# Turning the masks by DMA instead of on TensorE, and late one-hots in two full-width buffers, in a neighbour-maximum kernel

## What is computed

```python
h = maximum(layernorm(x), 0)
mask = adj != 0
vals, idx = top_k(where(mask, -arange(1024), -inf), 25)   # the first 25 neighbours of a row
feats = where(valid, h[idx], -inf)
agg = feats.max(axis=2)
agg = where(degree <= 25, maximum(agg, 0), agg)
out = x + relu(concat([h, agg]) @ W + b)
```

## Time and profile before

| | us |
|---|---|
| median of 3 runs | 699.37 (698.42 to 699.73) |
| the profiled execution | 697.45 |
| its span, first to last instruction | 695.7 |
| PE busy | 630.9 (91%) |
| DVE busy | 613.7 (88%) |
| ACT busy | 472.3 (68%) |
| POOL busy | 50.3 (7%) |

### The profile page before, as it was taken

One profiled execution on the slowest core, in us unless ns is written; L12 is line 12 of the kernel. 1 busy time (PEld: TensorE's weight loads), 2 busy tenths in 40 slices (PEclk: granted clock), 3 DMA queues, 4 the chain that ended last, 5 costly groups with the idle time before them and its releaser, 6 DMA issues.

```text
span 695.7 us, 10819 instructions
## 1 busy us (share of the span) xinstructions
PE 630.9 (91%) x3376; PEld 297.4 (43%) x3376; DVE 613.7 (88%) x813; ACT 472.3 (68%) x642; POOL 50.3 (7%) x41
## 2 busy tenths in 40 slices
PE   2479998999989999899999999899999999999976
PEld 2133443535445354443545344353535335353423
DVE  3368999899998999989998899989998899988997
ACT  2689478783777639775795947777497927959120
POOL 1300021000210002100030002100021000300000
...
GB/s 361 199 87 27 60 152 68 182 70 16 152 73 200 60 15 136 83 188 60 128 23 122 151 60 151 68 196 57 41 122 87 185 60 32 16 107 1 60 15 16
DMA packets 19127, 67.64 MB, mean 97 GB/s; under 512 B 4499, under 2 KB 7830, under 8 KB 16534
## 3 DMA queue, kind: packets, MB, share of 16 engines
...
## 4 chain that ended last, share of the span: by engine, by line
PE 66%; DVE 16%; issue 10%; ACT 4%; DVEq 1%; DMA 1%; POOL 1%; ACTq 0%
PE picked L506 18%; PE picked L507 17%; PE ring L455 14%; DVE late_hot L684 4%; PE side L469 4%; PE ring L449 4%; DVE hot L659 4%; PE side L463 4%; DVE best L775 3%; DVE best L678 3%; PE final L534 2%; PE final L538 2%; PE final L491 1%; DMA adj_in<-in_adj_dram 1%; DVEq L771 1%
## 5 line engine op out<-in xcount | busy, mean ns | idle before, releaser
L678 DVE TENSOR_TENSOR best<-picked,best 128x1024 f32<-128x1024 f32 x224 | 270.5, 1218 | 38.2 <-PE picked L507 36.0
L506 PE MATMUL picked<-hot,h_hi 128*128 128x512 f16 x512 | 194.5, 380 | 15.0 <-DVE best L775 7.5
L507 PE MATMUL picked<-hot,h_lo 128*128 128x512 f16 x512 | 194.0, 379 | 0.0
L506 PE MATMUL picked<-late_hot,hi_skew 128*128 128x512 f16 x336 | 127.6, 380 | 13.1 <-DVE late_hot L684 8.2
L507 PE MATMUL picked<-late_hot,lo_skew 128*128 128x512 f16 x336 | 127.3, 379 | 0.0
L344 ACT ACTIVATE late_rank<-ring,late_bias 128x512 bf16<-128x512 f32 x128 | 81.4, 690 | 57.6 <-PE ring L455 57.6
L775 DVE TENSOR_TENSOR best<-picked,best 128x1024 f32<-128x1024 f32 x84 | 102.4, 1219 | 8.3 <-PE picked L507 8.2
L378 ACT COPY best<-picked 128x1024 f32<-128x1024 f32 x32 | 32.2, 1013 | 102.6 <-PE picked L507 102.6
L659 DVE TENSOR_SCALAR hot<-rank 128x4096 f16<-128x4096 bf16 x64 | 89.4, 1399 | 12.0 <-ACT rank L344 12.0
L349 ACT ACTIVATE past<-side,bias_cut 128x512 bf16<-128x512 f32 x128 | 88.3, 690 | 6.2 <-PE side L469 4.9
L344 ACT ACTIVATE rank<-ring,bias_big 128x512 bf16<-128x512 f32 x128 | 83.1, 692 | 5.2 <-PE ring L455 4.9
...
## 6 DMA issues: line engine op xcount, KB each, us to landing
adj_in<-in_adj_dram SPq DMA_DIRECT2D x16, 2048.0 KB, 7.7
...
```

Source lines behind the costliest of these rows:

```text
L506: nc.tensor.matmul(dst, hi[:, slot, k, :], onehot, start=start, stop=False)
L507: return nc.tensor.matmul(dst, lo[:, slot, k, :], onehot, start=False, stop=stop)
L678: nc.vector.tensor_tensor(best[:, half, s, :, :], picked[s][:, :, :], best[:, half, s, :, :], ALU.max).then_inc(picked_read, 1)
```

## The change

The names and lines of the kernel after are some ten lines further down; what belongs together:

- **Masks by DMA.** The 32 PE transposes of a group and ACT's four copies go. ACT makes all four masks of a group in one go (`make_masks`), reading the int32 input with a stride of 8 elements so that the classes come out packed, and SP turns them with four transposing DMAs (`turn_masks`) into one of two buffers `mask_t`. The masks of group g+3 are made and turned in step g, one step earlier than before.
- **Places.** `lower_sums` moves from behind use 4 to the end of the step before it. The late ranks stand with uses 4 to 9 instead of 5 to 8, the prefix sums with 4 to 11, the ranks with 9 to 14, DVE's `count_rounds` behind take 11 instead of 9, the first late one-hot behind take 12 instead of 10 and 11.
- **Late one-hots.** They are full width (128 x 4096) and lie in two of four buffers `hot`. The one for round r+1 is made at the head of round r.
- **Prologue.** `x` is loaded first, then the first group's `adj` in four parts. DVE makes the first group's masks and the parts of `h` (before: ACT and POOL), and the masks of group 1 come from ACT.

```diff
-    LATE_WITH, PREFIX_WITH, RANK_WITH = spread_over(5, 8), spread_over(5, 12), spread_over(9, 13)
-
-    LATE_HOT_USES, COUNT_USE, MASK_USES = (10, 11), 9, (4, 9)
+    LATE_WITH, PREFIX_WITH, RANK_WITH = spread_over(4, 9), spread_over(4, 11), spread_over(9, 14)
+
+    LATE_HOT_USE, COUNT_USE = 12, 11
...
+    FIRST_RING = K
+    RING = 2 * K
+    LATE_AT, RANK_AT = 0, K
+    TURNED = 16 * Q
...
-            load_adj(0, 0)
+            masks_due = sp.alloc_register("sp_masks_due")
+            sp.reg_mov(masks_due, 0)
+
+            def turn_masks(slot):
+
+                sp.reg_add(masks_due, masks_due, Q)
+                for q in range(Q):
+                    sp.wait_ge(mask_made, q + 1)
+                    if q == 0:
+                        sp.wait_ge(mask_made, masks_due)
+                    sp.dma_start_transpose(mask_t[:, slot, :, q * P:(q + 1) * P],
+                                           mask[:, q, :, :].rearrange("p k j -> p (k j)")).then_inc(mask_turned, 16)
+
             load_x(0)
+            for q in range(Q):
+                sp.dma_start(adj_in[:, 0, q * N:(q + 1) * N], adj_v[0][:, q * N:(q + 1) * N]).then_inc(adj_first[q], 16)
             load_adj(1, 1)
             sp.dma_start(w_in[:, :, :], W.rearrange("(s p) n -> p s n", p=P)).then_inc(weights_loaded, 16)
             for i in range(3):
                 sp.dma_start(bias_in[i:i + 1, :], b.rearrange("(a n) -> a n", a=1)).then_inc(weights_loaded, 16)
             load_xres(0, 0)
-            for g in (0, 1):
-                sp.wait_ge(mask_made, Q * (g + 1))
-                load_adj(g + 2, g)
+            sp.reg_add(masks_due, masks_due, Q)
+            for q in range(Q):
+                sp.wait_ge(mask_made, q + 1)
+                sp.dma_start_transpose(mask_t[:, 0, :, q * P:(q + 1) * P],
+                                       mask[:, q, :, :].rearrange("p k j -> p (k j)")).then_inc(mask_turned, 16)
+            load_adj(2, 0)
+            turn_masks(1)
+            load_adj(3, 1)
             skew_h(0, 0)
             skew_late(0)
+            turn_masks(0)
...
+                if not at_end(it, u, 3):
+                    turn_masks((u + 1) % 2)
...
+                if isinstance(batch, int) and batch == 0:
+                    pool.wait_ge(mask_made, Q)
...
+            def make_masks(slot):
+
+                act.reg_add(turned_due, turned_due, TURNED)
+                act.reg_add(adj_due[slot], adj_due[slot], 16)
+                act.wait_ge(mask_turned, TURNED)
+                act.wait_ge(mask_turned, turned_due)
+                act.wait_ge(adj_loaded[slot], adj_due[slot])
+                for q in range(Q):
+                    counts = adj_in[:, slot, q * N:(q + 1) * N].bitcast(U32).rearrange("p (j k) -> p k j", k=K)
+                    nc.scalar.activation(mask[:, q, :, :], counts, ACT.Sign).then_inc(mask_made, 1)
...
-            relu_parts(0, 0)
...
+            stage(0, K - 1, rank[:, 0], bias_big[:, 0:1])
+            make_masks(1)
             turned_h(0, 0)
-            find_late(0, 0, FIRST_RING - TURNS)
+            find_late(0, 0, FIRST_RING)
...
+            make_masks(0)
...
-                    if use in MASK_USES and not at_end(it, u, 2):
-                        make_mask(MASK_USES.index(use), u % 2, 16 * (it * (UNROLL // 2) + u // 2 + 2), at)
...
-                if not at_end(it, u, 2):
-                    for q in range(len(MASK_USES), Q):
-                        make_mask(q, u % 2, 16 * (it * (UNROLL // 2) + u // 2 + 2), at)
...
-                if not at_end(it, u, 2):
-                    for n in range(TURNS):
-                        turned_mask(at + TURN_AT, n)
+                if not at_end(it, u, 3):
+                    make_masks((u + 1) % 2)
...
-            def turn_mask(g, at, n):
-                if n == 0:
-                    pe.wait_ge(mask_made, Q * (g + 1))
-                take(at + n)
-                for j in range(2):
-                    for q in range(Q):
-                        last = nc.tensor.transpose(ring16[n % 2][:, j, q * P:(q + 1) * P], mask[:, q, 2 * n + j::K], eye[:, :])
-                last.then_inc(ring_written, 1)
...
+            def lower_sums(g, half):
+
+                pe.wait_ge(mask_turned, TURNED * (g + 1))
...
+            def late_hot_of(turn, k):
+                return hot[:, bass.ds(1 + turn, 1), k, :]
...
+                    turn = nc.s_assert_within(r % 2, 0, 1, skip_runtime_bounds_check_because="a remainder of two")
+                    pe.wait_ge(late_hot_made, done + (r + (g + 1)))
...
-                        pe.wait_ge(late_hot_made[s], done + (r + (g + 1)))
                         pe.wait_ge(late_read[s], done + r + 1)
...
-                                last = pick(picked[s][:, j, :], hi_skew, lo_skew, k, late_hot[:, k, :], slot, i == 0, i == LINK - 1)
+                                last = pick(picked[s][:, j, :], hi_skew, lo_skew, k, late_hot_of(turn, k), slot, i == 0, i == LINK - 1)
                         last.then_inc(late_written[s], 1)
...
-                if not at_end(it, u, 2):
-                    turn_mask(g + 2, at + TURN_AT, 0)
                 if more:
                     pick_pair(g + 1, 2, next_slot)
+                    pick_pair(g + 1, 3, next_slot)
+                project(g, it, u, new_batch)
                 if not at_end(it, u, 2):
-                    turn_mask(g + 2, at + TURN_AT, 1)
-                if more:
-                    pick_pair(g + 1, 3, next_slot)
-                if not at_end(it, u, 2):
-                    turn_mask(g + 2, at + TURN_AT, 2)
-                    turn_mask(g + 2, at + TURN_AT, 3)
-                project(g, it, u, new_batch)
+                    lower_sums(g + 2, u % 2)
...
+            def first_mask(q):
+
+                dve.wait_ge(adj_first[q], 16)
+                nc.vector.tensor_scalar(mask[:, q, :, :], adj_in[:, 0, q * N:(q + 1) * N].rearrange("p (j k) -> p k j", k=K),
+                                        0.0, None, ALU.not_equal).then_inc(mask_made, 1)
+
+            def first_parts():
+
+                dve.wait_ge(normed_made, 1)
+                nc.vector.tensor_scalar(h_hi[:, 0, :, :], h32[:, :, :], 0.0, None, ALU.max).then_inc(h_made, 1)
+                dve.wait_ge(h_made, 1)
+                nc.vector.tensor_scalar(h32[:, :, :], h32[:, :, :], 0.0, None, ALU.max).then_inc(h_made, 1)
+                dve.wait_ge(h_made, 2)
+                nc.vector.tensor_tensor(h_lo[:, 0, :, :], h32[:, :, :], h_hi[:, 0, :, :], ALU.subtract).then_inc(lo_made, 1)
...
-                nc.vector.tensor_scalar(hot[:, (t - 1) % 3, :, :], rank[:, s, :, :], float(t), None,
+                nc.vector.tensor_scalar(hot[:, t - 1, :, :], rank[:, s, :, :], float(t), None,
...
-            def make_late_hot(i, which):
-
-                part = slice(i * HALF, (i + 1) * HALF)
-                nc.vector.tensor_scalar(late_hot[:, part, :], late_rank[:, part, :], which, None,
-                                        ALU.is_equal).then_inc(late_hot_made[i], 1)
+            def make_late_hot(turn, which):
+
+                nc.vector.tensor_scalar(hot[:, turn, :, :], late_rank[:, :, :], which, None, ALU.is_equal).then_inc(late_hot_made, 1)
...
-            for q in range(Q):
-                make_mask(q, 0, 16, None)
             stats_of(0, range(K))
             moments_of(0)
+            first_mask(0)
+            make_gain(0)
+            for q in range(1, Q):
+                first_mask(q)
...
-            make_gain(0)
-            for q in range(Q):
-                make_mask(q, 1, 16, TURNS)
-            dve.wait_ge(ring_read, FIRST_RING - TURNS)
-            make_hot(1, 0)
-            make_hot(2, 0)
...
+            first_parts()
+            dve.wait_ge(ring_read, FIRST_RING)
+            make_hot(1, 0)
+            make_hot(2, 0)
...
-                    if use in LATE_HOT_USES:
+                    if use == LATE_HOT_USE:
                         dve.wait_ge(ring_read, at + RANK_AT)
-                        make_late_hot(LATE_HOT_USES.index(use), numbers[:, 1:2])
+                        make_late_hot(1, numbers[:, 1:2])
...
-                    dve.wait_ge(ring_read, at + TURN_AT)
+                    dve.wait_ge(ring_read, at + RING)
                     make_hot(1, 1 - s)
...
+                    turn = nc.s_assert_within((r + 1) % 2, 0, 1, skip_runtime_bounds_check_because="a remainder of two")
+                    make_late_hot(bass.ds(1 + turn, 1), numbers[:, bass.ds(r + 2, 1)])
                     for i in range(2):
                         dve.wait_ge(late_written[i], done + r + 1)
                         nc.vector.tensor_tensor(best[:, s, i, :, :], picked[i][:, :, :], best[:, s, i, :, :],
                                                 ALU.max).then_inc(late_read[i], 1)
-                        make_late_hot(i, numbers[:, bass.ds(r + 2, 1)])
```

81 lines of the change are left out of this document (27 added, 54 removed).

## The result

The changed kernel took 745.55 us (median of 4 runs, 742.59 to 745.67), the kernel before beside it 698.89 us: a ratio of 1.066, 95% interval 1.063 to 1.069. It is slower, as predicted, but by 46.7 us where 10.9 were forecast, and outside the range.

What follows compares the result with a forecast made beforehand. Neither PE nor DVE alone was taken to bound it, but their alternating chain of waits. Steps +2.7, prologue -1.0 and +9.2, masks 0: span 695.7 to 706.6, time 710.3 us; 8-in-10 range 688 to 735.

Steps and rivals of the forecast that it cites:

- ACT's masks: Four strided masks at the end of ACT's step: 1.45 us apiece, hidden, so 0; bounds 0 and +16 us.
- cover: About 2.4 us of ACT's idle before the first late rank, hiding the four masks up to 1.57 us apiece.
- The rival: Strided masks slow ACT: at twice the time, 1.9 us apiece, 726 us; range 718 to 735, chance 0.12.
- Late one-hots: Full one-hots replacing halves on DVE: 58 x 0.19 = 11.0 us of work saved, rounds adding 0.4 idle with three.
- the wait at round 1: PE waits once in the late rounds, about 0.8 us, as round 1's one-hot stands ahead of round 0's take 0.
- Gaps close: Rival: DVE idles no more than before, under 0.6 us at take 10; 696.6 us, range 686 to 698, chance 0.22.
- Prologue: Before the first result: last rank 1.0 us earlier, then ACT's masks, transposes and skews delay the late ranks, +9.2 us.
- The waits and the places: DVE idles 1.1 us at take 4, 1.85 at 10, 0.37 at 11; PE waits 1.0 at use 15.
- the turns and the lower sums: Between use 2 and use 4: PE loses 2 us of transposes, gains 1.7 of lower sums; DVE idles 1.1.
- Transposes: Transposing DMAs: 6 us a group, issue 0.68 each on SP (bound 1.5), hidden in steps up to some 28 us.
- The slow rival: Transposing DMAs take far longer a group: 730 us at 16 us, about 870 at 34; 720 and far up, chance 0.10.

Runs made afterwards that it cites:

- n: Kernel before's places in the changed kernel, group 1's masks by DVE, two of ACT's four masks ahead of the copies in steps without a new batch: 691.6 us (0.991).
- o: n with the late one-hots undone, two of half width at uses 10 and 11, then one behind each take, in one buffer: 685.5 us (0.981).
- d: The changed kernel with late ranks, prefix sums, ranks and count at the places of the kernel before, late one-hot still at use 12: 707.2 us (1.011).
- l: The changed kernel with late ranks at uses 4 to 8 instead of 4 to 9 and DVE's count at use 9: 723.6 us (1.035).

## Why the prediction was right and wrong

The span came out 36.9 us above the forecast: 25.5 in the steps and 11.5 by the first result. Three terms of the sum are behind that.

**ACT's masks: the failed step.** The prediction took 0 for them, from the nearest row, a strided weight load at 1.5 times. The measured 2071 ns is 1.97 times. That is 15.5 us in 13 steps, about 0.9 more in the three steps where the clock fell, and 4.9 in the prologue: 21 of the 36.9. The working around the term held: cover up to 1.57 us apiece, four at 1.98 from start to start give 1.6 us a step, which is PE's 0.83 + 0.76; steps of three and four rounds lose that, odd ones 0.9. The rival named this mechanism, at 0.12. Its price, +16 us, was close for the steps and left out the prologue; its 718 to 735 us were missed too, since the two terms below were also too low. The Trainium skill (SBUF — State Buffer, Door 1: The DMA port swizzle) speaks against this read, with lines of 16 bytes; the trace agrees in direction, and puts the number at twice. I had weighed rule and row, and let the row of another engine decide.

**Late one-hots: wrong in sign.** In the sum they saved work (0.8 us with three rounds, 0.6 with two) and cost 0.4 and 0.3 of waits in the rounds, net 0.3 to 0.4 us less a step. By n and o they cost 0.4 to 0.5 more a step. That is 0.8 us off in each of 14 steps, 11 us; with the masks aside, the steps are 9 us over the forecast. It was measured with the places of before, so how much of the 9 it explains in the changed kernel isn't shown. The work saved was smaller than taken, 58 x 0.13 = 7.5 us instead of 11.0 (starts 1.19 apart at the loop, not 1.13). I had seen the wait at round 1 (0.7 to 0.95 in the traces) but not that the last takes move back. "Gaps close", which lived on this term, was never near: take 10 idled 1.80 us.

**Prologue: right chain, wrong sizes.** +8.2 against +19.7. The last rank came 0.6 us late. Between it and the first late rank lie 7.3 us more than worked out: masks 7.9 instead of 3.9, the issue of their transposes 5.4 instead of 2.7 (my 0.68 for one against 1.33, inside the bound of 1.5). And PE, idle for 11.3 us, had its clock lowered:

```profile
48.00:66.50 18.50, 6.39 (x21) 2.17 (x21) 4.71 (x4) 11.86 (x8) 0.00 (x0) 0.68 0.81 245
66.50:75.00 8.50, 8.50 (x27) 3.37 (x28) 4.62 (x4) 5.34 (x9) 0.00 (x0) 0.68 0.85 202
75.00:109.00 34.00, 30.96 (x149) 13.13 (x148) 30.25 (x33) 20.45 (x25) 0.00 (x0) 1.00 0.08 32
```

The granted clock is 0.68 on average to 75.0, between the levels of 1.2 and 2.4 GHz, and full behind it. At full clock the 8.5 us from 66.5 on would be some 2.7 shorter, an estimate from this row. The prediction had no term for it.

**The waits and the places: right.** The idle times came where and as large as worked out (0.98, 1.80, 0.29; PE waits 0.86 at use 15), and d and l show that the places cost time, at take 10 above all, as was said. Still, with the masks' length taken off, steps of two and three rounds are 40.5 and 41.6 us against 39.9 and 41.1. DVE's idle time in them, less the masks' length, is 3.4 and 4.8 us (3.3 and 5.2 predicted), the rest is 37.2 and 36.8 (36.6 and 35.9): what fell short is the saved work, not the waits. And half of the idle time at take 4, which was laid to the turns and the lower sums, is there only with the full one-hots (0.97 in n, 0.50 in o).

**Transposes: right.** I took 6 us for a group; the three issues ahead of the last and its landing make 3 x 1.33 + 3.3 = 7.3. The view holds all but the four of the first group, which stand behind the first loads and landed after up to 9.6 us:

```profile
L256 SPq DMA_TRANSPOSE mask_t<-mask x60: 1232/1326/1345, 45.1 to 632.8; - x60
...
DMA to landing us min/median/max: 3.1/3.3/4.7
```

The slow rival is out. The 1309 ns for a block of 128 x 128 that the Trainium skill gives (VectorE: DVE Perf Modes, The three transpose paths) would be, as an estimate by that page, 10.5 us for each of these, of eight blocks; the measurement decides, 3.3 us. No run here times a single block.
